# Moving the Q and V projections out of the attention stage, and loading the second batch's inputs before the first batch ends

## What is computed

```python
    Q = _split_heads(x @ WQ.T, h)
    K = _split_heads(x @ WK.T, h)
    V = _split_heads(x @ WV.T, h)
    scores = jnp.einsum('bhqd,bhkd->bhqk', Q, K) / jnp.sqrt(jnp.float32(dk))
    scores = jnp.where(causal, scores, NEG)
    ...
    attn = e / jnp.sum(e, axis=-1, keepdims=True)
    out = jnp.einsum('bhqk,bhkd->bhqd', attn, V)
    ...
    return out @ WO.T
x = _layernorm(x + _L0_attn_ref(...), axis=-1)
# ffn: RMS norm of x, quantised to 8 bits per row, times w_int8 * weight_scale, plus bias
x = _layernorm(x + _L0_ffn_ref(...), axis=-1)
```

## Time and profile before

| | |
|---|---|
| median of 3 runs | 1783.03 us |
| lowest and highest run | 1780.05 and 1798.64 us |
| the profiled execution | 1779.73 us |
| its span, first to last instruction, slowest core (core 0) | 1778.2 us |
| spans of the 8 cores | 1763.5 to 1778.2 us |
| TensorE matmul, busy | 1257.2 us, 71% |
| ScalarE, busy | 806.7 us, 45% |
| VectorE, busy | 663.1 us, 37% |
| GpSimd, busy | 305.1 us, 17% |
| mean granted TensorE clock, core 0 | 0.786 |

### The profile page before, as it was taken

One profiled execution on the slowest core, in us unless ns is written; L12 is line 12 of the kernel. 1 busy time (PEld: TensorE's weight loads), 2 busy tenths in 40 slices (PEclk: granted clock), 3 DMA queues, 4 the chain that ended last, 5 costly groups with the idle time before them and its releaser, 6 DMA issues.

```text
span 1778.2 us, 27745 instructions; the slowest of 8 cores (1763.5 to 1778.2 us)
## 1 busy us (share of the span) xinstructions
PE 1257.2 (71%) x8620; PEld 593.7 (33%) x8710; DVE 663.1 (37%) x1775; ACT 806.7 (45%) x1060; POOL 305.1 (17%) x599
## 2 busy tenths in 40 slices
PE   1997778767777776676509977797677777756664
PEld 0443334333444442222204423343334443422221
DVE  1332323212111137888703323232211111388886
ACT  0002244655778853444400022445556888434444
POOL 1003211221111111112210022212112111111212
PEclk9997789686656668888859977896766668788887
DMA  9330000300300001222292300002002000011211
GB/s 161 52 48 1 1 1 1 49 1 1 48 2 1 2 7 65 72 72 82 73 160 41 48 1 1 1 2 48 2 1 49 1 2 1 13 60 72 88 66 60
DMA packets 21927, 64.70 MB, mean 36 GB/s; under 512 B 1315, under 2 KB 1315, under 8 KB 21796
## 3 DMA queue, kind: packets, MB, share of 16 engines
q0 software_dynamic: 17184, 46.14, 13.2%
q1 hardware_dynamic: 4612, 16.78, 3.4%
HBM read 75.50 MB, written 16.78 MB: 52 GB/s over the span
## 4 chain that ended last, share of the span: by engine, by line
PE 45%; DVE 18%; ACT 12%; issue 9%; POOL 7%; DMA 7%; DVEq 1%; ACTq 0%; POOLq 0%
PE psall L266 14%; ACT PT L515 9%; PE psall L412 9%; PE psall L693 8%; PE psall L430 7%; PE psall L336 7%; POOL PT L566 6%; DMA wslotB<-wkt 5%; DVE o_ring L618 3%; DVE dump L731 2%; DVE dumpb L734 2%; DMA wslotB<-wvt 2%; ACT PT L526 2%; DVE OT L467 1%; DVE st L737 1%
## 5 line engine op out<-in xcount | busy, mean ns | idle before, releaser
L515 ACT ACTIVATE PT<-psall,ebias 128x1024 bf16<-128x1024 f32 x448 | 484.6, 1113 | 339.7 <-PE psall L412 333.0
L412 PE MATMUL psall<-QT,KT 64*128 64x512 bf16 (+3 forms) x1280 | 286.5, 447 | 158.2 <-DVE OT L467 39.4
L566 POOL TENSOR_TENSOR PT<-PT,mask 128x128 bf16<-128x128 bf16 x512 | 202.9, 425 | 849.2 <-ACT PT L515 759.7
L430 PE MATMUL psall<-Vx,PT 128*128 128x65 bf16 x4352 | 299.1, 217 | 57.8 <-POOL PT L566 49.4
L430 PEld LDWEIGHTS psall<-Vx,PT 128*128 128x128 bf16 x4352 | 212.8, 111 | 221.6 <-issue 206.4
L693 PE MATMUL psall<-wslotA,OT 128*128 128x512 bf16 x500 | 154.3, 476 | 82.7 <-DVE z L894 45.5
L605 DVE RECIPROCAL rinv<-psall 128x4 f32<-128x4 f32 x64 | 11.6, 181 | 465.1 <-PE psall L430 465.1
L266 PE MATMUL psall<-xT,wslotA 128*128 128x512 bf16 x475 | 155.4, 488 | 34.1 <-ACT PT L515 22.1
L266 PE MATMUL psall<-xT,wslotB 128*128 128x512 bf16 x502 | 115.5, 391 | 87.3 <-DMA wslotB<-wkt 86.7
L526 ACT ACTIVATE PT<-psall,ebias 128x768 bf16<-128x768 f32 (+2 forms) x192 | 129.2, 685 | 99.4 <-PE psall L412 96.1
L412 PEld LDWEIGHTS psall<-QT,KT 64*128 64x128 bf16 x1280 | 76.7, 97 | 277.5 <-issue 263.0
(11 more groups left out here) (94 smaller groups left out, 919.9 us busy)
## 6 DMA issues: line engine op xcount, KB each, us to landing
xstg<-x SPq DMA_DIRECT2D x32, 512.0 KB, 4.1
y<-outst POOLq DMA_DIRECT2D x32, 512.0 KB, 3.1
xT<-xt POOLq DMA_DIRECT2D x8, 1024.0 KB, 21.1
wslotB<-wkt POOLq DMA_DIRECT2D x2, 2048.0 KB, 41.7
wslotA<-wqt POOLq DMA_DIRECT2D x2, 2048.0 KB, 52.5
wslotB<-wvt POOLq DMA_DIRECT2D x2, 2048.0 KB, 16.8
wslotB<-w8t POOLq DMA_DIRECT2D x2, 2048.0 KB, 17.0
wslotA<-wot POOLq DMA_DIRECT2D x2, 2048.0 KB, 17.0
```

The lines of the kernel that those rows point to most:

```text
L412: last = eng.matmul(out, lhsT, rhs, start=True, stop=True, skip_group_check=True)
L430: last = eng.matmul(out, lhsT, rhs, start=(i_glob < 2), stop=(i_glob >= n_total - 2), skip_group_check=True)
L515: eng.activation(PT[:, pt * 1024:(pt + 1) * 1024], psall[:, p * 1024:(p + 1) * 1024], AF.Exp, bias=ebias[:, :], scale=0.125).then_inc(sem_ ...
L566: last = eng.tensor_tensor(blk, blk, mask01[:, :], ALU.mult)
```

## The change

There are three edits.

1. **Projections in one piece.** All 32 groups of Q come first (slot A), then all 32 of K (slot B), with `dt` as the outer loop. The results are copied to SBUF by ScalarE and no longer by VectorE. WV is loaded into slot A when Q is done, and the int8 weights into slot B when K is done.
2. **V at other places.** 8 groups of V stand ahead of block 0. The other 24 stand in block 0, three behind each of its 8 head pairs. Blocks 1 to 3 have no projection group.
3. **Early loads.** The second batch's WQ and 1792 of the 2048 columns of each `xT` tile are issued by GpSimd at tile 13 of the first batch's output part, when the output projection and the linear layer of tile 13 no longer need that memory. WK and the last 256 columns follow when the linear layer of tile 15 is done.

The diff, cut to this:

```diff
-            wk_done = wload(wk_h, 1, prev_t_end)
-            wq_done = wload(wq_h, 0, prev_t_end)
+            if pre is None:
+                wq_done = wload(wq_h, 0, prev_t_end)
+                wk_done = wload(wk_h, 1, prev_t_end)
+            else:
+                xt_done = pre["xt"]
+                wq_done = pre["wq"]
+                wk_done = pre["wk"]
...
-            for sch in range(4):
-                for dt in range(8):
-                    proj_group(1, dt, sch, KT, evK)
-            k_last_mm = ctr["t"]
-            wv_done = wload(wv_h, 1, k_last_mm)
-
-            W("t", wq_done[0], wq_done[1])
-            for dt in range(8):
-                proj_group(0, dt, 0, QT, evQ)
-            qrem = [(dt, sch) for sch in (1, 2, 3) for dt in range(8)]
...
+            for proj, (wdone, slot, dest) in enumerate(
+                    ((wq_done, 0, QT), (wk_done, 1, KT))):
+                W("t", wdone[0], wdone[1])
...
                 for dt in range(8):
+                    for sch in range(4):
+                        if half >= 4:
+                            W("t", "s", s_evac.get(half - 4))
...
+                        W("s", "t", mmv)
+                        def f3(eng, dt=dt, sch=sch, half=half, dest=dest):
+                            eng.copy(dest[:, dt * 2048 + sch * 512:
+                                          dt * 2048 + (sch + 1) * 512],
+                                     pslot(half)).then_inc(sem_s, 1)
...
+            wv_done = wload(wv_h, 0, q_last_mm)
...
+            w8_done = wload2(w8_h, 1, ctr["t"])
...
+            for g in range(8):
+                emit_vg(g)
+            vg_next = 8
...
-                        if qc == 0:
-                            vtarget = min(8, 2 * nst)
-                            qtarget = min(8, max(0, nst - 4) // 3)
-                        elif qc == 1:
-                            u1 = nst - 32
-                            vtarget = 8 + min(24, u1 // 2)
-                            qtarget = 8 + min(8, u1 // 6)
...
+                    if qc == 0:
+                        while vg_next < min(32, 8 + 3 * (hp + 1)):
+                            emit_vg(vg_next)
+                            vg_next += 1
...
             for i in range(NP):
                 VD(i)
+                if preload_cb is not None and i in (13, 15):
+                    preload_cb(i, wo_y2v, ffnv)
...
+            def preload_cb(i, wo_y2v, ffnv, nxt=nxt, bn=b + 1):
+                if i == 13:
+                    W("g", "t", wo_y2v[15])
...
+                    W("g", "t", ffnv[13])
+                    for c in range(4):
...
+                else:
+                    W("g", "t", ffnv[15])
...
```

More of the change, by code:

```diff
@@ L216, in ph0, with ph1, f @@
             return bump("v")
[L218 to L229, removed]
+        def ph1(b, v_ready, prev_t_end, prev_v_end, prev_s_end,
+                pre=None):
+            if pre is None:
+                W("g", "t", prev_t_end)
+                for c in range(4):
+                    def f(eng, c=c, b=b):
+                        src = ap(xt_h, b * D * S + (2 * c) * 128 * S,
+                                 (S, 128), (128 * S, 2), (1, S))
+                        dst = ap(xT, (2 * c) * 2048, (16384, 128),
+                                 (2048, 2), (1, 2048))
+                        eng.dma_start(dst, src).then_inc(sem_gx, 16)
+                    emit("g", f)
+                    bump("gx", 16)
+                xt_done = ctr["gx"]
             def wload(w_handle, slot, wait_t):
@@ L251, in pslot @@
+            s_evac = {}
+            v_evac = {}
+            half = 0
+            q_last_mm = 0
             def pslot(i):
                 return psall[:, (i % 4) * 512:((i % 4) + 1) * 512]
[L254 to L286, removed]
@@ L302, in ph1, with f @@
-            qrem = [(dt, sch) for sch in (1, 2, 3) for dt in range(8)]
[L303 to L310, removed]
+            for proj, (wdone, slot, dest) in enumerate(
+                    ((wq_done, 0, QT), (wk_done, 1, KT))):
+                W("t", wdone[0], wdone[1])
+                if proj == 0:
+                    W("t", "gx", xt_done)
+                    W("t", "v", v_ready)
+                    W("t", "v", prev_v_end)
+                    W("t", "s", prev_s_end)
+                for dt in range(8):
+                    for sch in range(4):
+                        if half >= 4:
+                            W("t", "s", s_evac.get(half - 4))
+                        def f(eng, dt=dt, sch=sch, half=half, slot=slot):
+                            out = pslot(half)
+                            for kt in range(8):
+                                lhsT = wslot[slot][
+                                    :, kt * 1024 + dt * 128:
+                                    kt * 1024 + dt * 128 + 128]
+                                rhs = xT[:, kt * 2048 + sch * 512:
+                                         kt * 2048 + (sch + 1) * 512]
+                                mm = eng.matmul(out, lhsT, rhs,
+                                                start=(kt == 0),
+                                                stop=(kt == 7),
+                                                skip_group_check=True)
+                                if kt == 7:
+                                    mm.then_inc(sem_t, 1)
+                        emit("t", f)
+                        mmv = bump("t")
+                        W("s", "t", mmv)
[3 more added lines that the diff above has]
+                                     pslot(half)).then_inc(sem_s, 1)
+                        emit("s", f3)
+                        s_evac[half] = bump("s")
+                        half += 1
+                if proj == 0:
+                    q_last_mm = ctr["t"]
@@ L390, in ph2, with emit_st @@
             trans_last_t = {}
[L391 to L399, removed]
+            for g in range(8):
+                emit_vg(g)
+            vg_next = 8
+            prev_evac = max(vones, v_upto[3])
+            def emit_st(qc, hp, k, p, wait_s):
+                W("t", "s", wait_s)
                 def f(eng, qc=qc, hp=hp, k=k, p=p):
@@ L474, in ph2 @@
                 for hp in range(8):
[L475 to L480, removed]
+                    if hp == 0:
+                        W("t", "v", v_upto[min(4 * qc + 3, 15)])
                     n_kt = 4 * qc + 4
```

108 lines of the change are left out of this document (57 added, 51 removed).

## The result

The changed kernel takes 1714.98 us (median of 8 runs, 1713.91 to 1718.62), the kernel before 1781.82 us (median of 8). The ratio is 0.9633, 95% interval 0.9619 to 0.9647: 67 us less. The prediction was 1763 us with a range down to 1733. The gain is four times the forecast one and outside the range, and the likeliest case, "just inside no change", was wrong.

A forecast was written before the change was run, and what follows sets the result against it. It took waits between steps in attention, and full DMA engines between the batches, to bound the kernel. Gains of 7.5 and 6.4 us in the batches plus 2.5 from early loads made 16.4: from 1779.7 to 1763 us, range 1733 to 1806.

The forecast's parts named there:

- just inside no change: Whole kernel: the forecast gain of 16.4 us lies within the 17.8 us (1%) a measurement can tell from no change.
- Block 3 and the output part keep their order and cost the same: Attention block 3 and the output part: no change in time; block 3 of the first batch stays at 159.5 us.
- I take these for all pairs of blocks 1 and 2: Attention blocks 1 and 2: each head pair without projection fill takes 10.76 and 15.48 us, 86.1 and 123.8 a batch.
- The price of dense groups: Projections: a group takes 1.73 us at full clock, 3.46 at half; the first 32 groups take 58.2 us.
- Part 1: Projections in one piece: Q 58.2 us, K 55.4 at full clock, with ScalarE's copies and the load of WV hidden.
- Rival C: Dense projections: not at full clock, at 0.87 costing 19 us a batch, 1801 us in all; chance 0.07.
- Part 2, V's chunks: Block 0: three V groups behind each head pair cost 5.2 us plus 1.7 lost to the clock; pair and chunk 12.2.
- rivals A and B: V chunks in block 0: at full clock, 1736 us, chance 0.18; or at half clock, 1819 us, chance 0.16.
- Part 3, early loads: Gap between batches: loads start 16.7 us earlier, but Q waits for all 8 MB; the second batch starts 2.5 us earlier.
- rival D: Gap between batches: loads hidden further, the second batch's Q starting at about 907, 1739 us in all; chance 0.09.
- The sum without the waits: Whole kernel: 13.9 us gained in the two batches plus 2.5 from early loads, 16.4 us in all.
- the bound of 5.5 us for the loads: Gap between batches: the most the early loads could gain, 5.5 us, if the stores of y cost nothing.

## Why the prediction was wrong

**The waits were not priced at all.** The step that failed is "Block 3 and the output part keep their order and cost the same", and with it "I take these for all pairs of blocks 1 and 2", 10.76 and 15.48 us. Both read durations of attention steps from the kernel before and carried them over, although the diff took four of six waits out of each step. Pairs of blocks 1, 2 and 3 take 10.2, 14.2 and 18.2 us. By the table that makes 28.7 us in the first batch, and 26.8 in the second by its own rows. Block 0 came out 2 us dearer than forecast in each batch, the gap 1 and the last output part 2, so that 48 us are left between 1763 and 1715. Some of the block 3 term is the slow block 3 of the core it was read from: by the medians of the eight cores that block gained 9.0 us in the first batch and 11.9 in the second. The experiments show the cause: without repeated waits the old order has the new step times, and with waits put back the new order loses them.

**The waits cost twice.** Four waits fewer shorten a step at half clock by 0.05 us, 0.8 us for the 16 steps of a pair of block 3. The pair lost 1.7. Part of the rest goes with the clock, as a step takes 1.10 us at half clock and 1.00 at full: from 0.64 to 0.80 the share of time at full clock rises by 0.3, so an estimate is 0.3 x 16 x 0.1 = 0.5 us. The remaining 0.4 stays open. By the medians of the eight cores, a pair of the first batch's block 3 lost 1.1 us, the clock rose from 0.72 to 0.80, and the two parts (0.8 and an estimate of 0.3) cover it. The clock in this block, by the same medians, was 0.50 with 6997 waits, 0.72 with 4621, 0.74 with 4437, 0.80 with 2005, and 0.77 to 0.79 with some 1230. So it falls as waits are added, but does not rise further below 2005. That the shorter steps are what lets the clock rise was not tried by itself.

**The price of dense groups** held: Q and K took 159.65 - 46.50 = 113.2 us for a forecast of 113.6, and the 8 groups of V 13.8.

**Part 1** held: ScalarE's copies were hidden, the projections stood at 1.00, WV caused no wait. Rival C, on the clock of the longer dense stretch, is out.

**Part 2, V's chunks** held in kind. 2.2 us were lost per chunk where 1.7 was taken, between the ends of 0 and 5.2; rivals A and B are out. That is the slowest core's first batch; where block 0 is shortest (first to last reciprocal 79.7 us) the loss is 79.7 / 7 - 5.3 - 5.2 = 0.9, so the 1.7 lies inside what the cores show. The time from pair to pair was (268.12 - 180.02) / 7 = 12.6 us for a forecast of 12.2 (180.02 is the first reciprocal of block 0).

**Part 3, early loads** was forecast at 2.5 us and gave nothing measurable. Its working was right (59.3 us for 58.4), and rival D is out. By the medians of the eight cores TensorE's idle time between the batches was 51.0 us before and 50.1 after.

**The sum without the waits** was 16.4 us. With equal waits the runs give 9.8 (lists of some 1230) and 22 (lists of 4437 and 4621, which differ by 184 waits). The forecast lies between the two. Two slips of the recorded working change little: the bound of 5.5 us for the loads leaves out the 0.6 us between landing and start (4.9), and the chance of 0.20 for "slower" is less than the 0.23 that B and C have together. What was argued from the order of work was sound, and it was the smaller part: two thirds or more of the 67 us came from a part of the diff that the prediction never named.

## What to carry to other kernels

Read a diff for its waits as for its matmuls, and before carrying a duration from one trace to another kernel check that its sequencer work is the same. Where semaphores only count up, as here, a wait for a value that the same engine has already waited for changes nothing in safety and can be left out by a few lines in the function that emits waits; here that was worth 74 us of 1782 on the kernel before, several times what the new order of its projections was worth. When a load is issued earlier but what it gates needs more bytes from the same full queue, the start does not move: put what gates the start first.

## What the runs showed that was not expected

- A wait of TensorE for a reached value costs from nothing (1536 of them ahead of 512-column matmuls: 2.5 us, within the intervals) over 18 ns (the first four added to each attention step) to some 60 ns (the next ones).
- The profile shows these waits, though not as waits: as idle time of TensorE under "issue" ahead of the scores, 134 times before, 166 with waits put back, 386 with many more, and in no row of the changed kernel or of the old order without repeated waits. Where steps ran at half clock they appeared only as 0.05 us between rows of matmuls.
- The granted clock of TensorE in the first batch's block 3, with the same matmuls, was 0.77 to 0.80 with up to 2005 waits, 0.72 to 0.74 with 4437 and 4621, and 0.50 with 6997, when the step at half clock had grown from 1.10 to 1.40 us (medians of the cores).
